# Second biases of the experts gathered into the routed rows instead of multiplied by the gates in the shared part

## What is computed

```python
def _L0_ffn_ref(x, gate_w, w1, b1, w2, b2, shared_w1, shared_b1, shared_w2, shared_b2):
    ...
    logits = xf @ gate_w
    top_logits, top_idx = jax.lax.top_k(logits, K)          # K = 2 of E = 8 experts
    top_gates = jax.nn.softmax(top_logits, axis=-1)
    gates = jnp.sum(jax.nn.one_hot(top_idx, E, dtype=xf.dtype) * top_gates[..., None], axis=1)
    h = gelu(jnp.einsum('nd,edh->neh', xf, w1) + b1)
    out_e = jnp.einsum('neh,ehd->ned', h, w2) + b2
    routed = jnp.einsum('ne,ned->nd', gates, out_e)
    shared = gelu(xf @ shared_w1 + shared_b1) @ shared_w2 + shared_b2
    return (routed + shared).reshape(B, S, D)
```

## Time and profile before

| | us |
|---|---|
| median of 3 runs (3273.34 to 3274.57) | 3274.34 |
| the profiled execution | 3277.38 |
| its span | 3275.6 |
| busy in it: TensorE, VectorE, ScalarE, GpSimd | 3175.7, 2173.6, 1267.7, 1051.4 |
| convolution, shared experts, routed experts end at | 642, 866, 1117 |

### The profile page before, as it was taken

One profiled execution on the slowest core, in us unless ns is written; L12 is line 12 of the kernel. 1 busy time (PEld: TensorE's weight loads), 2 busy tenths in 40 slices (PEclk: granted clock), 3 DMA queues, 4 the chain that ended last, 5 costly groups with the idle time before them and its releaser, 6 DMA issues.

```text
span 3275.6 us, 51687 instructions
## 1 busy us (share of the span) xinstructions
PE 3175.7 (97%) x18581; PEld 2699.7 (82%) x18581; DVE 2173.6 (66%) x5817; ACT 1267.7 (39%) x3058; POOL 1051.4 (32%) x1111
## 2 busy tenths in 40 slices
PE   7999999999999889999999999999998999999999
PEld 4666666689899769999999999999997788888887
DVE  6888888756555577778878787777776533333332
ACT  2333333333344345555555555555554311111111
POOL 7877777535211122222222222222201011010110
PEclk9999999999999899999999999999999999999999
DMA  4544443259644521111111111111101300000000
GB/s 129 155 142 133 132 140 95 81 171 313 194 155 151 207 90 53 46 46 46 46 46 40 39 46 46 46 39 40 46 14 44 108 26 26 26 26 26 26 14 13
DMA packets 123780, 267.41 MB, mean 82 GB/s; under 512 B 17689, under 2 KB 18337, under 8 KB 123530
## 3 DMA queue, kind: packets, MB, share of 16 engines
q1 hardware_dynamic: 100122, 186.59, 18.2%
q0 software_dynamic: 23408, 77.51, 7.0%
HBM read 159.49 MB, written 104.56 MB: 81 GB/s over the span
## 4 chain that ended last, share of the span: by engine, by line
PE 79%; DVE 9%; POOL 7%; ACT 1%; DMA 1%; issue 1%; SPq 0%; POOLq 0%; DVEq 0%
PE g_PH L1046 11%; PE g_O L1069 11%; PE t_U L1511 10%; PE t_S L1463 9%; PE t_PO L1498 5%; PE t_M L1447 5%; POOL c_kf L358 3%; PE t_T L1485 3%; PE f_Y L920 3%; PE f_Y L691 3%; PE t_M L1402 2%; PE f_Y L385 2%; PE f_Y L390 2%; DVE c_R L403 2%; DVE c_z L397 2%; PE t_M L1384 2%
## 5 line engine op out<-in xcount | busy, mean ns | idle before, releaser
L1473 ACT ACTIVATE t_pr<-t_sm,t_nb 128x256 f32<-128x256 f32 x512 | 256.5, 502 | 368.5 <-DVE t_nb L1469 368.5
L1059 DVE CAST g_hh<-g_hf 128x512 fp32r<-128x512 f32 x128 | 61.8, 483 | 434.7 <-PE g_O L1069 429.9
L1417 POOL TENSOR_TENSOR t_r<-t_r 128x256 f32<-128x256 f32 x128 | 95.9, 750 | 778.9 <-DVE t_rw L1479 451.7
L358 POOL TENSOR_TENSOR c_kf<-c_vt,c_ct 128x512 f32<-128x512 f32 x256 | 296.6, 1179 | 0.0
L1058 ACT ACTIVATE g_hf<-g_PH,g_b1s 128x512 f32<-128x512 f32 x128 | 88.2, 689 | 519.1 <-PE g_PH L1046 519.1
L1480 DVE TENSOR_SCALAR t_pr<-t_pr,t_rw 128x256 f32<-128x256 f32 x512 | 222.0, 434 | 18.2
L390 PE MATMUL f_Y<-c_kh,c_th 128*128 128x512 f32 x448 | 199.9, 446 | 9.6 <-ACT c_kh L365 9.6
L1046 PE MATMUL g_PH<-g_xh,g_w1h 128*128 128x512 f32 x512 | 205.3, 401 | 1.5 <-DVE g_xl L1034 1.5
L1046 PE MATMUL g_PH<-g_xh,g_w1l 128*128 128x512 f32 x512 | 203.0, 396 | 0.0
L1046 PE MATMUL g_PH<-g_xl,g_w1h 128*128 128x512 f32 x512 | 202.6, 396 | 0.0
L1069 PE MATMUL g_O<-g_w2h,g_hh 128*128 128x512 f32 x512 | 202.3, 395 | 0.0
(11 more groups left out here) (356 smaller groups left out, 9696.1 us busy)
## 6 DMA issues: line engine op xcount, KB each, us to landing
xs<-c_zero SPq DMA_DIRECT2D x71, 256.0 KB, 5.2
f_xg<-xs SPq DMA_DIRECT2D x71, 256.0 KB, 2.8
ys<-f_yt POOLq DMA_DIRECT2D x71, 256.0 KB, 2.4
c_tr<-kpad SPq DMA_DIRECT2D x60, 256.0 KB, 4.8
f_xg<-xn SPq DMA_DIRECT2D x40, 256.0 KB, 4.6
c_xt<-x SPq DMA_DIRECT2D x32, 256.0 KB, 3.5
c_cr<-ctx SPq DMA_DIRECT2D x32, 256.0 KB, 3.9
c_ct<-ctxh SPq DMA_DIRECT2D x32, 256.0 KB, 4.4
```

What stands on the lines that cost most here:

```text
L358: T["kv", h] = T["kv1", n] = p.do("gpsimd", lambda e: e.tensor_tensor(o, iv, ic, ALU.mult), g("vt", h), g("ct", h), g("kl", n - 8), g("kh" ...
L1473: T["ex", x] = p.do("scalar", lambda e, t=t, k4=k4: e.activation(pr[:, N % 2, t, :], sm[:, k4, :], ACT.Exp, bias=nb[:, k4, 0:1], scale=-1. ...
```

## The change

The gates are no longer multiplied by the second biases in the shared part: `gates`, `gates2`, the products of L687, gd, gt, gT, br and the last three operations of `choose` go, and a group's sums start with its first second product. In `setup` the table is loaded as [8, 2, 512] (the expert's bias beside the shared one), GpSimd adds the two, and SP writes the sum to a table eb of 8 rows in HBM; stg is not used for it any more. `experts` also writes en, the expert number of each tile in all 128 partitions. In the routed stage `bias2(j)` gathers row en[j] of eb into all 128 rows of buffer j % 4 of yt; it is issued by GpSimd two tiles ahead, and waits for the store that last read the buffer. The copy out of PSUM becomes an addition to that buffer. yt has four buffers in place of three; a gap of 544 floats keeps the places of the large weights.

```diff
@@ setup
-        U["c0",] = p.dma("sync", dc0, lambda e: e.dma_start(stg[0:73, 0, :], d["f0b2"]))
-        nst[0] = 1
-        U["wh", 0] = p.do("scalar", lambda e: e.activation(br[:, :], stg[0:73, 0, :], ACT.Copy), U["c0",])
-        U["br",] = U["wl", 0] = p.do("vector", lambda e: e.tensor_tensor(br[64:73, :], stg[64:73, 0, :], f32(br[64:73, :]), ALU.subtract), U["wh", 0], U["c0",])
-        a = p.do("gpsimd", lambda e: e.memset(gt[:, :, :], 0.0))
-        for z_ in (8, 40, 72):
-            U["g1",] = p.do("gpsimd", lambda e, z_=z_: e.memset(gt[:, :, z_:z_ + 1], 1.0), a)
+        U["c0",] = p.dma("sync", dc0, lambda e: e.dma_start(ob[:, :, :], d["f0b2"]))
+        a = p.do("gpsimd", lambda e: e.tensor_tensor(ob[:, 0, :], ob[:, 0, :], ob[:, 1, :], ALU.add), U["c0",])
+        U["ob",] = p.dma("sync", dc0, lambda e: e.dma_start(d["eb"], ob[:, 0, :]), a)
@@ choose
-        j1 = p.do("vector", lambda e: e.tensor_tensor(gd[:, r, :], oh[:, 0, r, :], gac[:, r, 0:1].to_broadcast(B8), ALU.mult), i_)
-        j2 = p.do("vector", lambda e: e.tensor_tensor(tb[:, :, :], oh[:, 1, r, :], gac[:, r, 1:2].to_broadcast(B8), ALU.mult), i_, gu("gd", c - 1))
-        U["gd", c] = p.do("vector", lambda e: e.tensor_tensor(gd[:, r, :], gd[:, r, :], tb[:, :, :], ALU.add), j1, j2)
@@ experts
+        U["en",] = p.do("vector", lambda e: e.tensor_copy(en, te), a)
@@ gates and gates2, and their calls, go
-    def gates(G):
-    def gates2(G):
...
@@ second1
-            if k == 0:
-                U["ob", G] = p.do("tensor", lambda e, o=o, c=c: e.matmul(O[o][:, :], gT[:, c], br[:, :], start=True, stop=False),
-                                  U["gl", G], U["gh", G], U["br",], gu("add", 2 * (G - 2) + t) if G > 1 else T["z1", 8 * n_heads - 4 + o], inc=t == 1)
...
-                tk = p.do("tensor", lambda e, a=a, b_=b_, o=o, fin=fin, c=c: e.matmul(O[o][:, :], a[:, n % 2, c], sw2[b_][:, k, :], start=False, stop=fin),
-                          U["hh", n], U["hl", n], U["sw2", k], inc=(q == 2 and (t == 1 or fin)))
+                tk = p.do("tensor", lambda e, a=a, b_=b_, o=o, fin=fin, c=c, beg=k == 0 and q == 0: e.matmul(O[o][:, :], a[:, n % 2, c], sw2[b_][:, k, :], start=beg, stop=fin),
+                          U["hh", n], U["hl", n], U["sw2", k], (gu("add", 2 * (G - 2) + t) if G > 1 else T["z1", 8 * n_heads - 4 + o]) if k == 0 else None, inc=(q == 2 and (t == 1 or fin)))
@@ before the routed stage
+    keep.sb("gap", [128, 544])
...
-    yt = keep.sb("yt", [128, 3, 512])
+    yt = keep.sb("yt", [128, 4, 512])
@@ routed stage
+    def bias2(j):
+
+        U["yb", j] = p.dma("gpsimd", dv[j % 4], lambda e: e.indirect_dma_start(
+            out=yt[:, j % 4, :], out_offset=None, in_=d["eb"], in_offset=bass.IndirectOffsetOnAxis(ap=en[:, j:j + 1], axis=0)),
+            gu("ys", j - 4), U["en",], U["ob",], U["o2", steps - 1])
+
@@ second2
-        U["y", j] = p.do("vector", lambda e: e.tensor_copy(yt[:, j % 3, :], O[s][:, :]), U["m2", j], gu("ys", j - 3), U["o2", steps - 1])
-        U["ys", j] = p.dma("gpsimd", dy[j % 3], lambda e: e.dma_start(ysv[j], yt[:, j % 3, :]), U["y", j])
+        U["y", j] = p.do("vector", lambda e: e.tensor_tensor(yt[:, j % 4, :], yt[:, j % 4, :], O[s][:, :], ALU.add), U["m2", j], U["yb", j])
+        U["ys", j] = p.dma("gpsimd", dy[j % 4], lambda e: e.dma_start(ysv[j], yt[:, j % 4, :]), U["y", j])
@@ the loop over n of the routed stage, between turnh and second2
+        if LAG - 2 <= n < TILES + LAG - 2:
+            bias2(n - LAG + 2)
```

More of the change, by code:

```diff
@@ L138, in front_phase @@
     et = keep.sb("et", [1, TILES], I32)
+    en = keep.sb("en", [128, TILES], I32)[:, :]
     bt = keep.sb("bt", [128, 2, TILES])
@@ L143, in front_phase @@
     b1s = keep.sb("b1s", [128, 4])
-    br = keep.sb("br", [73, 512], F32R)
-    gd = keep.sb("gd", [128, NT, 8])
-    gt = keep.sb("gt", [128, 2, 73])
     idc = keep.sb("idc", [128, NT, 2], I32)[:, :, :]
@@ L155, in front_phase @@
     xr = keep.sb("xr", [128, 2, 512])
-    gT = keep.sb("gT", [73, 256], F32R)
     low = ExitStack()
@@ L208, in front_phase @@
     sm = m.sb("sm", [128, 2, 8, 8])
-    tb = m.sb("tb", [128, 8, 8])
     ne = m.sb("ne", [128, 8])[:, :]
@@ L215, in front_phase @@
     rb = m.sb("rb", [8, 256])[:, :]
+    ob = m.sb("ob", [8, 2, 512])
     pad = m.sb("pad", [128, 3688])
@@ L648, in turn1 @@
         U["xl", G] = U["PR",] = p.do("vector", lambda e: e.tensor_tensor(lo, src, f32(hi), ALU.subtract), a, *old)
-    def gates(G):
-        for z_ in (0, 32, 64):
-            U["gc", G] = p.do("vector", lambda e, z_=z_: e.tensor_copy(gt[:, :, z_:z_ + 8], gd[:, 2 * G:2 * G + 2, :]), U["gd", G // 4], gu("gp", G - 1), U["g1",])
-    def gates2(G):
-        a = U["gc", G]
-        for t in range(2):
-            b_ = p.do("tensor", lambda e, t=t: e.transpose(PL[0:73, 128 * t:128 * t + 128], gt[:, t, :], ident), a, gu("PV"), inc=t == 1)
-        a = U["gp", G] = b_
-        U["gh", G] = a = p.do("scalar", lambda e: e.activation(gT[:, :], PL[0:73, 0:256], ACT.Copy), a, gu("ob", G - 1))
-        U["gl", G] = U["PV",] = p.do("vector", lambda e: e.tensor_tensor(gT[32:41, :], PL[32:41, 0:256], f32(gT[32:41, :]), ALU.subtract), a)
     def first1(G, k):
@@ L770, in front_phase @@
                         loadr(lb)
-                    if lb == 0:
-                        gates(0)
                     if lb in (1, 2):
                         turn1(lb - 1)
-                    if lb == 3:
-                        gates2(0)
     assert not left and not shared and not ahead
@@ L824, in front_phase @@
                         scatter(row(i))
-                if k == 2:
-                    gates2(G + 1)
-        if n < steps and k == 1 and G + 1 < NG:
-            gates(G + 1)
         if n < steps and k in (1, 2) and 2 * G + 3 + k < NT:
@@ L854, in front_phase @@
     hl2 = keep.sb("hl2", [128, LAG + 1, 2, 128], F32R)
-    yt = keep.sb("yt", [128, 3, 512])
+    yt = keep.sb("yt", [128, 4, 512])
     over = U["mm1", NG - 1]
     dl = [p.dsem(f"l{i}") for i in range(4)]
-    dy = [p.dsem(f"y{i}") for i in range(3)]
+    dy = [p.dsem(f"y{i}") for i in range(4)]
+    dv = [p.dsem(f"v{i}") for i in range(4)]
     PT2 = (PM, PL)
@@ L1691, in layouts @@
     a["rb1"] = c(i["L0_ffn_b1"])
-    b2 = np.zeros((96, 512), np.float32)
-    for z in (0, 32, 64):
-        b2[z:z + 9] = np.concatenate([i["L0_ffn_b2"], i["L0_ffn_shared_b2"][None]])
-    a["f0b2"] = b2[:73]
+    a["f0b2"] = c(np.stack([i["L0_ffn_b2"], np.tile(i["L0_ffn_shared_b2"], (8, 1))], 1))
     a["gw"] = c(i["L0_ffn_gate_w"].reshape(4, 128, 8).transpose(1, 0, 2))
@@ L1723, in program @@
         d[n] = nc.dram_tensor(n, (B, S, D), F32, kind="Internal").ap()
+    d["eb"] = nc.dram_tensor("eb", (NE, D), F32, kind="Internal").ap()
     d["tok"] = nc.dram_tensor("tok", (B * S, 4), F32, kind="Internal").ap()
```

## The result

The changed kernel takes 3268.99 us (median of 20 runs, 3265.95 to 3270.74) against 3275.44 us for the kernel before on the same chip (20 runs): the medians differ by 6.5 us. The ratio over all runs is 0.9978 with an interval of 0.9972 to 0.9985; taken on 3275.44 it makes the change 7.2 us faster, 4.9 to 9.2. The profiled execution took 3268.49 us, its span 3266.7 us against 3275.6.

A forecast was written before the change was run, and what follows sets the result against it. TensorE, with work for 97% of the span, was taken as the bound. Terms -10.7 - 2.7 + 0.9 + 2.6 = -9.9 us gave 3264.4 us from a median of 3274.34; range 3259.5 to 3271, the forecast's own 3261.5 to 3267.5.

The forecast's parts named there:

- Gate products and their waits in the shared stage: Shared stage: products and transposes taken off TensorE save 10.7 us; the wait for VectorE's copies at 671.56 saves 1.6 us.
- The DMA rival: Shared stage from 720 us: DMA engines at 0.95 set the pace, 5.5 us lost, -4.4 us, 3269.9 us; chance 0.17.
- The wait at 642.71 and L653: Before the shared products: wait for bank PV at 642.71 goes, 0.9 us; copies no longer delay L648's split, 0.2 us.
- VectorE's choosing: Convolution: nine small VectorE operations go, about 1.0 us of VectorE; taken as zero gain, at most 1.0 us.
- Setup: Kernel start: GpSimd loses memsets and gains a 1.26 us addition that delays the first products; costs 0.9 us.
- Routed stage, steady part: Routed tiles: gathers landing in 3.5 us within 8.5 us of lead, tiles still 3.48 us; cost 0.
- The gather rival: Routed stage: additions wait for gathers landing at 9.6 us, tiles of 3.83 us, +24 us, 3288 us; chance 0.10.
- End of the routed stage: Last tiles: GpSimd's queue of gathers and stores makes tile 70's addition and the last store late; costs 2.6 us.
- the prediction's own sign of it: Start or seam to attention: the prediction would be wrong if either takes more than 3 us.

The follow-up runs named there:

- the last experiment: Kernel before without the three VectorE operations per choosing that fill the gate table, which GpSimd zeroes once instead; 3273.65 us beside 3273.81 for the kernel before.
- the two moved tensors: Kernel before with an unused tensor: 284 bytes per partition ahead of the first biases, 3278.36 us; or 832 bytes ahead of the routed weights, 3274.82 us.

## Why the prediction was right, and where its steps were not

The forecast was 3264.4 us, -9.9; the runs say 7.2 us faster (4.9 to 9.2), and the ratio taken on the first median, 3274.34, gives 3267.1 us. The main mechanism was as predicted and the sum came near, but partly by luck: the end of the routed stage with its seam cost 7.7 us more than predicted, and the rest gained 6.7 us more in the pair of profiles. About 3 of these 6.7 are the drops of the clock. For the terms I use all kernels, not the one profile, where a stretch is the same in several; they add up to some -5 us, at the low end of the interval, so one or two microseconds stay unplaced.

- *Gate products and their waits in the shared stage: predicted -10.7 - 1.6 = -12.3, measured about -11.* The profiled execution of the changed kernel had the stage at 202.0 us (-13.6), but the eight variants that share it had 202.1 to 207.0, and all nine have a mean of 204.2; the kernel before and its four variants 214.1 to 215.6, mean 215.3. This is why the spans differ by 8.9 and the medians by less. Two things make the scatter. Drops of the clock, 1.7 us each: one in the changed kernel and five variants, two in the three others; two in the kernel before and two of its variants, one in the other two. And TensorE's waits, next point. Without the drops, and where TensorE waits for nothing from 700 to 830 us, the stage is 200.3 to 200.5 us in three kernels against 212.0 to 212.4 in four: -11.8, near the -12.3. A group from 707 us on takes 12.83 us before ((796.97 - 707.19) / 7 at L661) and 12.11 after ((785.72 - 713.08) / 6 at L653): 0.72 us less, 0.70 predicted.
- *The DMA rival there.* From 720 to 800 us the share in windows of 20 us was 0.93 to 0.99 in the changed kernel and its eight variants, but for two of 0.90, mostly above the 0.95 that the rival took for the limit, and a group got shorter by 0.72 us, so its strong form (5.5 us lost) is wrong. TensorE's waits from 700 to 830 us, none in the changed kernel and two variants, are 0.7 to 2.3 us in the other six, 1.1 on average over the nine; in the kernel before and its four variants they are none but for 0.6 in one. That fits a stage near its DMA limit, but nearly all of these waits are put down to VectorE, and no run took transfers away. How far the transfers set them stays open; the price is about 1 us.
- *The wait at 642.71 and L653 (-1.1), VectorE's choosing (0, at most -1.0): measured together -3.3.* The first part is as costed: what the last experiment leaves of the gap is 1.2 us. The second was mis-sized, twice. I had sized nine operations by three small copies, 0.32 us, as 1.0 us, where a choosing's three take 0.6 and the nine 1.8, and called them hidden since TensorE had idle time. But TensorE waited 3.1 us at L490 for c_xb in the trace of before, in three places, and I did not look whose list that wait ends in. They cost about 2 us, twice the "at most".
- *Setup (+0.9): measured +1.0.* The addition on 8 partitions took 1.25 us, my 1.26 from the 128-partition row:

```profile
22.38 1.25 POOL L422 TENSOR_TENSOR c_ob<-c_ob 8x512 f32<-8x512 f32 x1
...
27.43 0.77 PE L387 MATMUL f_Y<-c_kh,c_th 128*128 128x512 f32 x1 [10.46 <-ACT c_kh L362]
```

  The first value product starts at 27.2 us on average in the seven kernels that have the addition there (26.7 to 27.7), at 26.2 in the kernel before and its four variants; the loads of the start vary by half a microsecond, and the profile's +1.3 contains that.
- *Routed stage, steady part (0): the gathers cost nothing, and about 2 us came from elsewhere.* Their landing had a median of 4.3 us, not 3.5, well inside the 8.5 us of lead. The period fell from 3.476 to 3.447 us, with the gathers and without them, most likely for the reason of the two moved tensors, over 66 tiles 1.9 us. The other 1.4 us of the -3.2 are the drop of the clock at 865. No step of the prediction asked what the change does to addresses, or what the clock does to a stage.
- *The gather rival.* Every gather but those of the crowded end was in time. The Trainium skill, "SBUF — State Buffer", section "A bandwidth-pool intuition that's wrong (but worth ruling out)", gives about 22.5 GB/s per port, from which the prediction made an estimate of 11.7 us for one row behind one port. The trace doesn't agree with that use of it: 262,144 B in 4.3 us are 61 GB/s, from an expert's single 2 KB row in nearly every tile.
- *End of the routed stage (+2.6, at most 5.9): measured +8.2, and +2.1 at the seam.* This is the step that failed, and the prediction's own sign of it came true: end and seam to attention together took 10.3 us more, where it allowed 3. It said that the crowd was over by then, from the 2.28 us of the last store, so it took single landings of 3.5 and 2.3 us and no queue that was late already. The crowd starts 17.5 us ahead of the last first product in both kernels (1070.9 of 1088.4). In the changed kernel it finds a queue in which a gather waits for a store four tiles back; stores landed in up to 7 us, not 2.4, and GpSimd was late before the drain began. And the drain itself was worked out with a store landing of 2.3 and a gather of 3.5 us; with 3.6 and 4.4, as measured with the crowd spread, it costs 5.7 us instead of 2.6 (14.7 against 9.0). The crowd adds 2.5 more, together 8.2. The 2.1 us at the seam, from the last addition to attention's last gathered row, are there in every kernel with gathers (16.3 to 17.1 us, but for the one that held the loads, where it is longer) and not in the six without (14.2 to 15.1). The profiles place them: from the last store's issue to the first gather's 3.87 us instead of 3.19, the first gather's issue 1.73 instead of 1.01, the last one's landing 7.44 instead of 6.75. Why each is longer stays open.

## What to carry to other kernels

A prefetch that is free while an engine is the bound is paid for in the drain, where tiles come at the pace of the last product alone: cost the loop over the buffers there (load landing, operation, store landing, divided by the number of buffers), with landings read from the most crowded stretch and not from the last transfer. Buffers whose readers have ended by the drain are the cheap way out, but only together with a queue that isn't already late. An engine with idle time doesn't hide an operation on another: look for a wait of the first that ends in the second's list at that place.

## What the hardware showed that I hadn't expected

- A matmul of 256 columns took 277, 280, 281 or 284 ns on average, in three kernels that differ in nothing but where the tensors lie in SBUF: 3.435 to 3.478 us for a tile. A difference of this size between two kernels is no evidence on the edit.
- 128 reads of one 2 KB row landed in 4.3 us (median), issued at 0.97 us of GpSimd; stores beside them went from 2.4 to 3.4 us in the steady part (medians) and up to 7.0 us in a crowd of 412 GB/s.
- The granted clock fell to 1.2 GHz for about 3.4 us at a time, once or twice in the shared stage of every kernel here, 1.7 us each. Two profiles of kernels with the same stage differ by that alone, so read the granted clock in short stretches before you put such a difference down to an edit.
- An addition of 8 x 512 on GpSimd took 1.25 us, one of 128 x 512 1.26 us.
